# Attention layer 1 of a graph network block: queries and keys on 32-column tiles, scores in two steps, ELU in two column parts

## What is computed

```python
xr = jnp.einsum('nd,rdf->rnf', x, W)          # 3 relations
oi, oj = xr[etype, dst], xr[etype, src]
alpha = jax.nn.leaky_relu(oi @ q + oj @ k, 0.2)
m = jax.ops.segment_max(alpha, dst, num_segments=n_nodes)
e = jnp.exp(alpha - m[dst])
a = e / (jax.ops.segment_sum(e, dst, num_segments=n_nodes)[dst] + 1e-16)
out = jax.ops.segment_sum(a[:, :, None] * oj.reshape(-1, heads, out_ch), dst, ...) + b
# layer 1 -> elu -> layer 2
```

## Time and profile before

| | us |
|---|---|
| median of three runs | 1082.29 |
| lowest and highest run | 1080.98, 1083.15 |
| profiled execution | 1082.61 |
| its span, first to last instruction | 1080.9 |
| TensorE busy | 1038.2 (96%) |
| VectorE busy | 766.2 (71%) |
| ScalarE busy | 574.5 (53%) |
| GpSimd busy | 263.1 (24%) |
| mean granted TensorE clock | 0.995 of full |

### The profile page before, as it was taken

The page is one execution under the profiler, slowest core; times in us unless marked ns, Lnnn a source line. Parts: engine busy times, 40 slices in busy tenths (PEclk is TensorE's granted clock), DMA queues, the critical chain, the costliest instruction groups (busy, mean ns, idle before and its releaser), DMA issues.

```text
span 1080.9 us, 17705 instructions
## 1 busy us (share of the span) xinstructions
PE 1038.2 (96%) x7436; PEld 856.5 (79%) x7436; DVE 766.2 (71%) x1099; ACT 574.5 (53%) x610; POOL 263.1 (24%) x160
## 2 busy tenths in 40 slices
PE   6999999999999999999899989999999999999997
PEld 5899987445689984545879679966999999999994
DVE  8793855888754237888554484745998989989873
ACT  0432316888633338888224373234767676766650
POOL 3424804889400027988100000000000000000000
PEclk9999999999999999999999999999999999999999
DMA  8033247222042374221424302512978787878750
GB/s 297 13 117 148 89 131 233 66 60 69 2 176 88 121 228 139 59 65 35 153 96 176 117 1 88 203 57 94 323 243 295 236 298 238 290 248 283 255 178 32
DMA packets 82292, 163.20 MB, mean 151 GB/s; under 512 B 4044, under 2 KB 60136, under 8 KB 81918
## 3 DMA queue, kind: packets, MB, share of 16 engines
q1 hardware_dynamic: 80736, 151.86, 41.4%
q0 software_dynamic: 1472, 10.15, 3.3%
HBM read 158.35 MB, written 0.80 MB: 147 GB/s over the span
## 4 chain that ended last, share of the span: by engine, by line
PE 79%; DVE 13%; issue 3%; ACT 2%; POOL 1%; DVEq 0%; POOLq 0%; ACTq 0%
PE PS L1091 20%; PE PS L773 8%; PE PS L944 7%; PE PS L789 5%; PE PS L695 5%; PE PS L582 5%; PE PS L1074 4%; PE PS L512 4%; PE PS L671 4%; PE PS L525 3%; PE PS L594 3%; PE PS L1107 2%; PE PS L1009 2%; PE PS L831 2%; DVE PRD L1690 1%
## 5 line engine op out<-in xcount | busy, mean ns | idle before, releaser
L1943 DVE TENSOR_TENSOR Wlo<-W,Whi 128x2304 fp32r<-128x2304 f32 x68 | 172.1, 2551 | 19.0 <-ACT Whi L1438 19.0
L1438 ACT CAST Whi<-W 128x2304 fp32r<-128x2304 f32 x68 | 144.5, 2127 | 0.2 <-DMA W<-in_L_rel 0.2
L1091 PE MATMUL PS<-Whi,Mhi 128*128 128x384 f32 x408 | 138.1, 338 | 0.0
L1091 PE MATMUL PS<-Wlo,Mhi 128*128 128x384 f32 x408 | 136.6, 335 | 0.0
L1091 PE MATMUL PS<-Whi,Mlo 128*128 128x384 f32 x408 | 136.5, 335 | 0.0
L479 POOL TENSOR_TENSOR PRDP<-arena 128x1024 f32<-128x1024 f32 x48 | 114.7, 2390 | 30.2 <-issue 17.8
L773 PE MATMUL PS<-QH,SEL 128*128 128x512 f32 x384 | 115.9, 422 | 5.2 <-ACT xT L1269 1.4
L1290 ACT ACTIVATE arena<-PS 128x1024 f32<-128x1024 f32 x96 | 98.5, 1026 | 23.6 <-PE PS L773 23.6
L773 PEld LDWEIGHTS PS<-QH,SEL 128*128 128x128 f32 x384 | 64.8, 188 | 55.2 <-DVE PRD L1690 21.3
L1290 ACT ACTIVATE PS<-PS 128x1024 f32<-128x1024 f32 x96 | 97.9, 1020 | 2.6 <-PE PS L773 2.6
L1091 PEld LDWEIGHTS PS<-Whi,Mhi 128*128 128x128 f32 x408 | 76.8, 188 | 0.4 <-DVE Wlo L1943 0.2
(11 more groups left out here) (302 smaller groups left out, 2429.1 us busy)
## 6 DMA issues: line engine op xcount, KB each, us to landing
W<-in_L_rel SPq DMA_DIRECT2D x68, 1152.0 KB, 6.3
W<-in_W_rel SPq DMA_DIRECT2D x6, 2304.0 KB, 8.7
W<-in_W SPq DMA_DIRECT2D x6, 2304.0 KB, 9.2
arena<-in_qU SPq DMA_DIRECT2D x96, 128.0 KB, 2.7
W<-in_WqT SPq DMA_DIRECT2D x4, 2304.0 KB, 9.3
W<-in_W_root SPq DMA_DIRECT2D x2, 2304.0 KB, 13.5
W<-in_WgT SPq DMA_DIRECT2D x2, 2304.0 KB, 9.8
QH<-QH POOLq DMA_DIRECT2D x2, 1536.0 KB, 9.9
```

Source lines behind the costliest of these rows:

```text
L1091: mm = pe.matmul(PS[:, 4 + s % 2, 0:HALF], MS[a][mb][:, k, j * P:(j + 1) * P], WS[b][w % 3][:, k, :], start=n == 0, stop=n == 17)
L1438: nc.scalar.copy(WS[0][w % 3][:], W[(FIRST34 + r) % 2][:, :, q * HALF:(q + 1) * HALF]).then_inc(w_hi, 1)
L1943: V.tensor_tensor(WS[1][w % 3][:], W[(FIRST34 + r) % 2][:, :, q * HALF:(q + 1) * HALF], WS[0][w % 3][:].bitcast(F32), ALU.subtract).then_i ...
```

## The change

Ten edits, all in the attention layers:

1. `qk1` is widened from 8 to 32 columns, with zeros behind the 8 factors. GpSimd fills it with zeros first, and makes `pick` (128 x 8, a unit matrix in each 32 partitions, by two fills and four selects in all with `qk1`'s). `qkR` gets 128 partitions.
2. `queries_keys(r)`: chunk k goes to the 32-column tile k % 4 of the array and so to partitions 32(k % 4) on; chunks 4 and 5 add to tiles 0 and 1. Four partial sums lie on 128 partitions. Banks are 3 and 2 instead of 3 and 4.
3. `spread_keys` and `turn_queries` multiply with `pick`, which adds the four partial sums; the second is a plain fp32 matmul into bank 1 instead of a transpose, one part for relations 0 and 1 and one for relation 2.
4. TensorE's order: queries and keys 0 and 1 together, parts 6 and 7 of turn 2, spread relations 0 and 1 of head 0, turn their queries, part 8, queries and keys 2, wait, spread and turn relation 2, spread head 1.
5. VectorE copies relations 0 and 1 of `qkR` ahead of its copies of parts 6 and 8; `qkN` is copied in two parts.
6. ScalarE makes the scores of relations 0 and 1 for units 0 and 1 first, relation 2's after.
7. `weighted_sum(5)` goes ahead of `turn_probs(6)`.
8. ELU in two column parts: the first 576 columns (heads 0 to 2) of both tiles after head_out(5), the last 192 of each tile after head_out(6) and head_out(7).
9. VectorE's third 10 moves to layer 2, behind `rows_lo_turned(1)`.
10. The scaling of `QKB` goes behind that.

```diff
-        qk1 = sb("qk1", [P, KC, 2 * HEADS1])
+        qk1, pick = sb("qk1", [P, KC, HQ]), sb("pick", [P, 2 * HEADS1])
-        qkR = put("qkR", [2 * HEADS1, R3 * NODES], F32, 36)
+        qkR = put("qkR", [P, R3 * NODES], F32, 36)
...
-            pool.dma_start(qk1[:], turned(A["qk1"])).then_inc(small_in, 16)
+            then(nc.gpsimd.memset(qk1[:], 0.0))
+            then(nc.gpsimd.memset(pick[:], 0.0))
+            for j in range(4):
+                v = pick[HQ * j:HQ * j + HQ]
+                then(nc.gpsimd.affine_select(out=v, in_=v, compare_op=ALU.not_equal, fill=1.0, base=0,
+                                             pattern=[[-1, 2 * HEADS1]], channel_multiplier=1))
+            pool.dma_start(qk1[:, :, 0:2 * HEADS1], turned(A["qk1"])).then_inc(small_in, 16)
...
-                    mm = pe.matmul(PS[0:2 * HEADS1, 3 + r // 2, (r % 2) * NODES:(r % 2 + 1) * NODES], qk1[:, k, :], XT[:, r, k, :],
-                                   start=k == 0, stop=k == KC - 1)
+                    j = k % 4
+                    mm = pe.matmul(PS[HQ * j:HQ * j + HQ, 3 - r // 2, (r % 2) * NODES:(r % 2 + 1) * NODES], qk1[:, k, :], XT[:, r, k, :],
+                                   start=k < 4, stop=k + 4 >= KC)
...
-            def turn_queries():
+            def turn_queries(rs):
-                for c in range(R3 * NT):
-                    r, t = divmod(c, NT)
-                    mm = pe.transpose(PS[:, 6, 2 * HEADS1 * (R3 * t + r):2 * HEADS1 * (R3 * t + r + 1)],
-                                      qkR[:, c * P:(c + 1) * P], ident[0:2 * HEADS1, 0:2 * HEADS1])
+                for r, t in product(rs, range(NT)):
+                    mm = pe.matmul(PS[:, 1, 2 * HEADS1 * (R3 * t + r):2 * HEADS1 * (R3 * t + r + 1)],
+                                   qkR[:, (NT * r + t) * P:(NT * r + t + 1) * P], pick[:], start=True, stop=True)
                 mm.then_inc(rows_turned, 1)
...
                     queries_keys(0)
-                    turn_rows(2)
                     queries_keys(1)
-                    queries_keys(2)
+                    turn_rows(2, (0, 1))
...
-                for h in range(min(H, 2)):
-                    spread_keys(h)
-                    if l == h == 0:
-                        turn_queries()
+                if l == 0:
+                    spread_keys(0, range(R3 - 1))
+                    turn_queries(range(R3 - 1))
+                    turn_rows(2, (2,))
+                    queries_keys(2)
+                    pe.wait_ge(qkr_copied, 2)
+                    spread_keys(0, (R3 - 1,))
+                    turn_queries((R3 - 1,))
+                    spread_keys(1)
+                else:
+                    spread_keys(0)
                 keep_busy(30 if l == 0 else 52, 7)
                 for i in range(2 * H):
+                    if i == 2 * HEADS1 - 2:
+                        weighted_sum(u0 + i - 1)
                     turn_probs(u0 + i)
...
-                    if i:
+                    if i and i != 2 * HEADS1 - 2:
                         weighted_sum(u0 + i - 1)
...
-                scores(u0)
+                if l == 0:
+                    for t in range(NT):
+                        scores(t, range(R3 - 1))
+                    scores(0, (R3 - 1,))
+                else:
+                    scores(u0)
...
-                    for t in range(NT):
-                        act.wait_ge(elu_min, t + 1)
-                        nc.scalar.activation(xT[:, 3 * t:3 * t + 3, :], MT[0][:, 3 * t:3 * t + 3, :], ACT.Exp).then_inc(elu_exp, 1)
+                    for i, cols in enumerate((early_cols, late_cols)):
+                        for t in range(NT):
+                            act.wait_ge(elu_min, NT * i + t + 1)
+                            nc.scalar.activation(flat_rows(xT, t)[:, cols], flat_rows(MT[0], t)[:, cols], ACT.Exp).then_inc(elu_exp, 1)
...
                 if l == 1:
+                    rows_lo_turned(1)
+                    third_lo(10)
                     dve.wait_ge(qkb_in, 16)
                     then(V.tensor_scalar(QKB, QKB, -1.0, None, ALU.mult))
-                    rows_lo_turned(1)
...
+                    if x == "r2" and l == 0:
+                        dve.wait_ge(qk_done, 2)
+                        V.tensor_scalar(qkR[:, 0:2 * NODES], PS[:, 3, :], -1.0, None, ALU.mult).then_inc(qkr_copied, 1)
...
+                    dve.wait_ge(rows_turned, 1)
+                    V.tensor_copy(qkN[:, :, 0:R3 - 1, :], turned_queries[:, :, 0:R3 - 1, :]).then_inc(qkn_copied, 1)
                     dve.wait_ge(qk_done, 3)
-                    V.tensor_scalar(qkR[:, 2 * NODES:], PS[0:2 * H, 4, 0:NODES], -1.0, None, ALU.mult).then_inc(qkr_copied, 1)
...
+                    V.tensor_scalar(qkR[:, 2 * NODES:], PS[:, 2, 0:NODES], -1.0, None, ALU.mult).then_inc(qkr_copied, 1)
+                    dve.wait_ge(rows_turned, 2)
+                    V.tensor_copy(qkN[:, :, R3 - 1, :], turned_queries[:, :, R3 - 1, :]).then_inc(qkn_copied, 1)
...
-                    head_out(2 * H - 2)
-                    elu(0)
-                    head_out(2 * H - 1)
-                    elu(1)
+                    for t in range(NT):
+                        elu_start(t, 0, early_cols)
+                    for t in range(NT):
+                        elu_end(t, 0, early_cols)
+                    for t in range(NT):
+                        head_out(2 * H - 2 + t)
+                        elu_start(t, 1, late_cols)
+                        elu_end(t, 1, late_cols).then_inc(att_done, 1)
```

More of the change, by code:

```diff
@@ L898, in _, with turn_rows @@
             keep_busy(4, 3)
-            def turn_rows(r):
+            def turn_rows(r, js=range(3)):
                 pe.wait_ge(xr_copied, r + 1)
-                for j in range(3 * r, 3 * r + 3):
+                for j in (3 * r + i for i in js):
                     if j >= 2:
@@ L970, in _, with spread_keys @@
                 if l == 0:
-                    pe.wait_ge(qkr_copied, 2)
+                    pe.wait_ge(qkr_copied, 1)
                 else:
                     pe.wait_ge(qk_made, 2 * R3 * NT)
-                def spread_keys(h):
+                def spread_keys(h, rs=range(R3)):
                     if h >= 2:
                         pe.wait_ge(score_done, u0 + 2 * h - 2)
-                    for r in range(R3 if l == 0 else 0):
+                    for r in rs if l == 0 else ():
                         mm = pe.matmul(PS[:, 4 - h % 2 * 2 + r // 2, (r % 2) * NODES:(r % 2 + 1) * NODES],
-                                       ident[0:2 * HEADS1, HEADS1 + h:HEADS1 + h + 1].to_broadcast([2 * HEADS1, P]),
+                                       pick[:, HEADS1 + h:HEADS1 + h + 1].to_broadcast([P, P]),
                                        qkR[:, r * NODES:(r + 1) * NODES], start=True, stop=True)
@@ L1384, in _, with scores @@
                         rows_out(r)
-                if l == 0:
-                    act.wait_ge(qkn_copied, 1)
-                else:
+                if l == 1:
                     act.wait_ge(qk_made, 2 * R3 * NT)
-                def scores(u):
+                def scores(u, rs=range(R3)):
                     h, t = divmod(u - u0, NT)
-                    act.wait_ge(key_spread, u0 // 2 + h + 1)
+                    if l == 0:
+                        act.wait_ge(key_spread, h + 1 if h == 0 and R3 - 1 not in rs else h + 2)
+                        act.wait_ge(qkn_copied, 2 if R3 - 1 in rs else 1)
+                    else:
+                        act.wait_ge(key_spread, HEADS1 + 2)
                     if u >= 2:
                         act.wait_ge(exp_done, u - 1)
-                    for r in range(R3):
+                    for r in rs:
                         ins = nc.scalar.activation(SC[u % 2][:, r * NODES:(r + 1) * NODES],
@@ L1406, in turned_probs @@
                                    ).then_inc(pt_copied, 1)
-                scores(u0)
+                if l == 0:
+                    for t in range(NT):
+                        scores(t, range(R3 - 1))
+                    scores(0, (R3 - 1,))
+                else:
+                    scores(u0)
                 for u in range(u0, u0 + 2 * H):
                     if u + 1 < u0 + 2 * H:
-                        scores(u + 1)
+                        scores(u + 1, (R3 - 1,) if u == 0 else range(R3))
                     act.wait_ge(max_ready, u + 1)
@@ L1833, in _ @@
                 if l == 1:
+                    rows_lo_turned(1)
+                    third_lo(10)
                     dve.wait_ge(qkb_in, 16)
                     then(V.tensor_scalar(QKB, QKB, -1.0, None, ALU.mult))
-                    rows_lo_turned(1)
-                order = [2, 3, 4, 5, 6, "r0", 7, 8, "r1", 9, "r2", 10]
-                for x in order:
+                for x in [2, 3, 4, 5, 6, "r0", 7, 8, "r1", 9, "r2"]:
                     if isinstance(x, int):
@@ L1895, in head_out, with elu_start, elu_end @@
```

(14 more changed lines are left out.)

12 lines of the change are left out of this document (6 added, 6 removed).

## The result

The changed kernel takes 1076.12 us (median; 1075.8 to 1076.79) against 1082.28; the ratio is 0.9941 (0.993 to 0.9953). The forecast was 1077.6, with 1076.1 as its low end: the sign was right and the front came as forecast, the gain was 6.2 us instead of 4.7, and by the ratio the time (0.9941 x 1082.29 = 1075.9) lies just under the range. The profiled execution took 1076.79 us around a span of 1075.0.

The account below looks back on a forecast made before the run. The prediction took attention layer 1 as a relay, its loop paced by VectorE between chains of waits. Front 4.5 + back 0.45 - fillers 0.15 - mode change 0.1 = 4.7 us gain, so median 1077.6, range 1076.1 to 1080.0.

Parts of the forecast that it names:

- Tiles: Queries and keys in attention layer 1: six matmuls of one relation on four tiles take 0.9 us instead of 2.69.
- Front: Chain from layer 1's last product to the first row maximum: the loop begins at 615.2 instead of 619.7, gain 4.5 us.
- What could be late next: The 30 fillers ahead of the loop may end late at the low clock: 0.15 us put down as loss.
- The first rival: TensorE's low clock falls elsewhere, at 612 to 616 or in the loop: gain 3.1 us, time 1079.2; chance 0.15.
- gain 4.85: Remark on TensorE's clock: plain matmuls for the queries' turnings would rather keep it up, gain 4.85 us; no chance given.
- The rival that prices the fall inside TensorE's part: Low clock on relation 2's matmuls, spreading and turning, or in the loop: up to 1.6 us lost; chance 0.15.
- Changes of mode: Front of attention layer 1: changing the array's width costs 0.1 us, with one change on the path.
- Back: Behind the loop, moved weighted sum 5 and ELU by columns: tile 0's turning at 653.3 instead of 653.74, gain 0.45 us.
- Costed at nothing: GpSimd's fills, selects and factor load, and VectorE's low part 10 moved to layer 2: all fit into idle time, 0 us.
- Sum: Whole kernel: front, back, late fillers and mode change together gain 4.7 us, median 1077.6.
- The two bounds named for the low end: Range's low end 1076.1: 0.67 us for the tiles (0.6 less in all) and a gain of 1.0 at the back.
- The rival without overlap: The four tiles don't run side by side: 2.69 us stays, loop begins at 620.2, 0.5 later, time 1082.3; chance 0.06.

Follow-up runs that it names:

- e13: The kernel before, unchanged, first of three further profiles of it: 1083.17 us, stage 54.5 us in all three.
- e4: The changed kernel, unchanged, timed and profiled again: 1075.75 us, against 1082.99 for the kernel before on the same chip.
- e6: The kernel before with 16 fillers instead of 30 between the spreading and the loop: 1082.45 us, ratio 1.0002.
- e1: The changed kernel with all six matmuls of each relation on the first 32-column tile, one behind the other: 1083.5 us, ratio to before 1.0004.
- e5: The changed kernel with each relation's six matmuls one behind the other, their factors four times in 128 columns of weights: 1083.94 us.
- e8: The changed kernel with turning 6 ahead of weighted sum 5 again: 1075.91 us.
- e9: The changed kernel with ELU in one piece per tile again, the moved weighted sum kept: 1076.44 us.
- e10: The changed kernel with low part 10 at the front again and the factors' scaling back ahead of layer 2's low parts: 1076.8 us.
- e16: The changed kernel with relations 0 and 1 serial on one tile, relation 2 on four: eight runs 1079.7 to 1080.4 us, four 1084.2 to 1084.7.

## Why the prediction missed

- **Tiles.** 0.9 us a relation was forecast; 1.85 for two and 1.08 for the exposed one were measured. Right.
- **Front.** 4.5 forecast, 13.89 - 9.28 = 4.61 measured. Spreading 0.90 (0.9), turning four blocks 0.79 (0.85), part 8 0.50 (0.66), relation 2's copy 0.43 (0.46), the last score 0.48 (0.41). Right, within 0.16 each.
- **What could be late next: the step that failed.** "I put 0.15 down for it" took the low clock as a loss that might remain. It was a loss of the kernel before that the change removes. The three later profiles have a stage 1.25 us longer than the profile used, all of it behind slow fillers; against them the changed stage is 6.7 us shorter, not 5.45. Between the spans of e13 and e4 lie 6.9 us, these 6.7 and 0.2 behind the stage. The medians on one chip are 7.2 apart; the remaining 0.3 has no trace. In the profile used, the low clock cost nothing (front and loop are those of e6), so that loss could not be read from it. The first rival had the clock in another place; that it would not fall at all had a sentence (gain 4.85) and no chance, and even there its worth was put at 0.15. The rival that prices the fall inside TensorE's part at up to 1.6 us was right about the price: 1.5 in e1. The prediction's reason for 4.85, plain matmuls instead of transposes for the queries, is not what keeps the clock up: e1 and e5 have the same plain matmuls, and the clock fell.
- **Changes of mode: the second step that failed.** A loss of 0.1 us was forecast. They turned out a gain of 0.38 in the loop: spreading from 8 partitions was itself a change of mode, twice, and the earlier trace rows showed the slow sum behind it, 2.16 against 1.95 to 1.97 elsewhere. Nor was the change of width new: in the kernel before, the turning behind relation 0's 8-column sums starts 0.31 us after the last of them, as behind the 32-column sums of the changed kernel, where 0.22 is the step inside the sums. Wrong sign.
- **Back.** 0.45 forecast. From sum 1's head_out to tile 0's turning 18.36 us against 18.49 before, so 0.13; and 0.32 at tile 1, whose turning follows the fillers without a gap. The sum is right, the split isn't. The moved sum costs 0.25 (e8), the columns give 0.77 (e9), each by one profile; I had the moved sum as what makes the early columns possible.
- **Costed at nothing.** GpSimd's fills and selects take some 3.5 us (the prediction's 2 had no row behind it) and leave 16.67 of its 20.43 us of idle time; low part 10 delays nothing in layer 2, where the product goes on without a wait, and would cost 0.5 in front (e10). Right.
- **Sum.** By the two first profiles 5.9: 4.61 + 0.39 + 0.13 + 0.32 in the stage, 0.45 around it, where other runs of either kernel differ by as much (the last product ends anywhere from 604.7 to 605.8). Of the 1.2 us between these 5.9 and the forecast 4.7, the mode changes are 0.5, the part around the stage 0.45, the 0.15 put down for the fillers was not lost, and the front is 0.1. The back agrees with its term. That leaves the clock out: it comes in only against the other profiles of the kernel before.
- **Slips in the sums.** Twelve instructions at 0.46/8 are 0.69 us, not 0.67. The two bounds named for the low end give 1077.6 - 0.6 - 0.55 = 1076.45, not 1076.1, and hold nothing for the clock. The rival without overlap has the loop 3 x 1.8 = 5.4 us later, at 620.6 and not at 620.2; e1, without its 1.5 us of low clock, is 0.7 us behind the kernel before.

What makes the clock fall is not settled. The amount of serial fp32 sums goes with it (none of 8 profiles without them, 9 of 9 with all three relations, a third of the runs in e16), the weights' width doesn't, and bf16 fillers between them only put it off. That the sums are the cause is not shown. The Trainium skill ("TensorE: Matmul & The Clock Gate", What's actually happening) says that recent busyness sets the clock. Here TensorE was busy for 12.75 of 13.6 us ahead of the fall, and in the changed kernel for 8.69 of 10 us with no fall behind it, so the busy time of a profile doesn't tell when it falls.

## What to carry to other kernels

Small fp32 matmuls with few columns of weights belong on separate column tiles when they stand in a chain of waits: twelve of them (24 instructions) took 1.85 us instead of 5.3. Read the granted clock in more than one profile of the kernel before, since a stretch at a half, even where it seems covered, is a term of the sum with both signs. Fillers that don't end in time at the half clock become the wait (30 of them took 5.93 us and held the loop up); but fewer are no sure gain, since with 16 the median stayed and four of eleven runs came out 2.5 us later at a lower mean clock. Before a change of mode is priced as a loss, look for the ones that the kernel has already: a matmul on 8 or 32 partitions between others on 128 is one.

## What the runs showed of the hardware

- A change of the array's mode costs 0.19 us each way where 8 or 32 rows follow 128 and back inside the loop (before, e1 and e16 against the changed kernel), and 0.15 and 0.10 in the front of e1; from 128 to 32 columns it costs 0.12 us and back 0.15 (e1 against e5).
- Four fp32 matmul instructions on four 32-column tiles start within 0.02 us of each other, and the next four start 0.22 us later (changed kernel); on one tile it is one instruction every 0.22 us (e1).
- Low clock comes in stretches of 3 to 10 us (e1 has the shortest, e16 the longest), and its place shifts between runs of one kernel; e16 has two groups of runs 4.3 us apart, both of one program.
- A GpSimd select over 32 x 8 elements takes 0.74 us (2.96 for four), while the fill of 128 x 192 takes 0.28.
